# A layered mixture-of-experts and attention kernel: zero fills placed earlier in SP's queue, and the order of scores, value products, maxima and quotient in the attention loop

## The chip, the cores and the metric

The kernel runs on one core of one Trainium2 chip. The metric is the device time of one execution in microseconds (us). A core has five engines with a queue of instructions each: TensorE (PE in the profile, with its weight loads as PEld), VectorE (DVE), ScalarE (ACT), GpSimd (POOL) and SyncE (SP). SP does no arithmetic here; it issues transfers, which 16 DMA engines carry out. Engines wait for each other by semaphores.

## The reference, cut to what matters

There are 32 sequences of 128 tokens with 128 channels, so 4096 tokens, and a condition vector of 64 values for each sequence. Two layers follow each other, each with a residual:

```
x = x + ffn0(cond0(x, cond))     # cond0: channels scaled by the condition, a product, clip
x = x + ffn1(cond1(x, cond))     # cond1: adapter 128 -> 32 -> 128 with conditioned weights
ffn0: router, the best 2 of 8 experts (silu gated, width 176), and a shared expert
ffn1: h = layernorm(x); q, k, v = h @ w_qkv
      scores = q k / sqrt(8), 16 heads of 8 channels;  attn = softmax(scores)
      x = x + (attn v) @ w_o + b_o
      h = layernorm(x); router, the best 2 of 8 experts (relu, width 512)
      x = x + experts
```

## The kernel before, in words

The program has five stages, one after the other: `layer0` (condition, shared expert and router of the first layer, 0 to about 115 us), `experts0` (the first layer's routed experts, to 237), `pre_attention` (adapter, layer norm, q, k, v, to 306), `attention` (with the second router, to about 545), and `experts1` (to the end). All are written engine by engine: each stage has one function for each engine, and the order of its queue is the order of the calls there. Nothing is planned by a scheduler.

**Routing through DRAM.** A router writes each token's row into a DRAM buffer of 8 regions, one for each expert (`dispatch_rows` for the first layer, `late_rows` for the second), by scatters from GpSimd. The experts then read tiles of 256 rows, in 39 tiles. As the last tile of an expert is not full, unused rows must be zero. `fill_region` (L404) writes zeros over one region of `late_rows` with two DMAs of 1040 KB on SP's queue, and `fill_dead` (L415) over what lies past the regions with one. Of the 8 regions, `layer0` fills the first six (`EARLY_FILLS`, L399 to L412, called at L559), and SP fills the last two in `attention`, at pairs 2 and 3 (L1656). The semaphore `m.filled` counts all of them. GpSimd waits for the full count at lap 10 of `attention` (L1706), before its first scatter into `late_rows`.

**The end of `experts0`.** For each tile SP loads the rows and the weights (L1002, L1004). GpSimd scatters the expert's result rows into `expert_rows` (L948, `send_rows`). A tile may take its result buffer only when the scatters of four tiles before have landed (L932). Behind the last tile's loads SP issues two loads of the adapter's gains (`gbu`, L1006; the trace names them `eg`) and then calls `fetch_halves` (L855): it waits for the scatters that concern the first half of `expert_rows`, loads it into V with four DMAs of 512 KB, waits for the rest, and loads the second half into X3 with four more (L865). VectorE waits for all four loads of V, adds V onto X in eight instructions (L956), and adds X3 for the first two groups of four sequences (L964). Then the stage ends for all engines, and the first instruction of TensorE in `pre_attention` (L1339) can start.

**The attention loop.** One lap handles one sequence s; a lap runs over four groups g of four heads. In lap s TensorE does, for each g:

* `score(s + 2, g)` (L1884): masked keys times queries, for the maxima;
* `shift(s, g)` (L1894 and L1896): keys times queries again, minus the maximum, for the exponent;
* at g = 0 `mix(s - 1)` (L1914): the value products, 32 small matmuls into psO; at g = 3 `total(s - 1)` (L1923): the sums of the exponents, 32 more;
* at g = 0 the ranks for the router, once in four laps (`post_rank`, L266); at g = 1 `turn_max(s + 1)` (L1902), a transpose of the maxima, or at g = 2 in the lap with `routing`; at g = 2 or 3 `project(s - 2)` (L1933).

VectorE takes the maxima (`maximum`, L1735, four a lap), spreads them (`spread_max`, L1741), computes the reciprocal of the sums (`invert`, L1747), the quotient (`divide`, L1752) and the residual (`keep`, L1756). The score banks are two, so `score(s, g)` waits for the maximum of g - 2. GpSimd splits the maxima into two parts (`part_max`, L1680 and L1682), masks keys (`mask_k`, L1670), spreads values (`spread_v`, L1690) and scatters rows (L358). ScalarE takes the exponents (L1833) and masks keys (L1826).

**Norm and router** of a group of four sequences run in pieces in later laps, so every fourth lap has the same piece. Six laps behind: VectorE's moments, gather and variance (L1450, L1458, L1466) and GpSimd's root (L1473). Seven: offset, norm and its transpose. Eight: GpSimd's join (L1480), the product for the router (L1522). Nine ("routing"): logits and the choice of experts on VectorE. Ten ("placing"): ranks, slots and the index (L339), then GpSimd's scatters, two a lap for four laps.

SP's queue in `attention` loads queries and keys a pair of sequences at a time (`load_pair`, L1129, three buffers) and the masked queries (`load_masked`, L1594), each behind a wait for `shifted`.

Of the kernel before, what the change touches and what calls it, by code (L numbers as in the profile page):

```python
# [17 lines left out]
SEQS = 32  # L18
# [4 lines left out]
E = 8  # L23
# [377 lines left out]
EARLY_FILLS = 6  # L401


def fill_region(m, sp, e):  # L404


    tiles = TOK // SLOTS // FILLS
    rows = m.tail[:, e].rearrange("p a c -> p (a c)").unsqueeze(1).to_broadcast([P, tiles, 2 * ROW])
    for f in range(FILLS):
        at = e * REGION + f * tiles * SLOTS  # L410
        sp.dma_start(m.xbufs[1][at:at + tiles * SLOTS].rearrange("(i p a) c -> p i (a c)", p=P, a=2), rows
                     ).then_inc(m.filled, 16)  # L412
# [444 lines left out]
def fetch_halves(m, sp, sent, layer):  # L857


    for a, to in enumerate((m.V, m.X3)):  # L860
        sends_done(m, sp, sent, layer, a)
        mine = m.ybuf[a * TOK:(a + 1) * TOK, :].rearrange("(p s) c -> p s c", s=SEQS)
        for h in range(HALVES):
            part = slice(h * HS1, (h + 1) * HS1)
            sp.dma_start(to[:, part, :], mine[:, part, :]).then_inc(m.rows_in[1 + h] if a else m.rows_in[0], 16)  # L865
# [101 lines left out]
def experts0(m, d):  # L967

    nc = m.nc
    with ExitStack() as ctx:  # L970
# [4 lines left out]
        s = [sb(f"es{q}", [HALF, 2, SLOTS]) for q in range(2)]  # L975
# [15 lines left out]
        with nc.Block(no_gpsimd_drain=True) as block:  # L991
            @block.sync
            def _(sp):
                for n, b, i in rounds(sp, ETILES, EB, head=EB, tail=EB - 1):
                    if isinstance(n, int) and n < LEAD:
                        continue
                    e = sp.value_load(m.table[0:1, bass.ds(n, 1)], min_val=0, max_val=E - 1)
                    row = sp.value_load(m.table[0:1, bass.ds(n + ETILES, 1)], min_val=0, max_val=E * REGION + (E - 1) * SLOTS)
                    hold(m, sp, down, n - EB + 1)
                    hold(m, sp, copied, n - EB + 1)  # L1000
                    hold(m, sp, evac, n - EB + 1)
                    sp.dma_start(xs[b][:], m.xbufs[0][bass.ds(row, SLOTS), :].rearrange("(a p) c -> p a c", p=P)  # L1002
                                 ).then_inc(ld[b], 16)
                    sp.dma_start(w[b][:], d["W123"][bass.ds(e, 1)].rearrange("e p h -> (e p) h")  # L1004
                                 ).then_inc(ld[b], 16)
                for b in range(2):  # L1006
                    sp.dma_start(gbu[b][:], m.gb_dram[b * GT:(b + 1) * GT, 2 * DOWN:].unsqueeze(0).to_broadcast(
                        [DOWN, GT, 2 * P])).then_inc(m.gbu_in[b], 16)
                fetch_halves(m, sp, st, 0)

            @block.tensor
# [515 lines left out]
def post_logits(q, dve, n, b, banks):  # L1527

    route_logits(q.router, dve, n, b, banks, q.nat)
# [74 lines left out]
def attention(m, d):  # L1604
# [3 lines left out]
    with ExitStack() as ctx:  # L1608
# [33 lines left out]
        with nc.Block(no_gpsimd_drain=True) as block:  # L1642
            @block.sync
            def _(sp):
                for k in range(PAIRS):
                    ahead = k + 1
                    if 2 <= ahead < PAIRS:
                        if ahead >= PAIR_BUFFERS:
                            sp.wait_ge(shifted, HG * 2 * (ahead - PAIR_BUFFERS + 1))
                        if ahead % 2 == 0:  # L1650
                            sp.wait_ge(m.qk_out[ahead // 2 % 2], 16 * (ahead // 4 + 1))
                        load_pair(m, sp, ahead, ahead % PAIR_BUFFERS)
                    if k >= 2:
                        sp.wait_ge(shifted, HG * 2 * (k - 1))
                        load_masked(m, sp, k)
                    if k in (2, 3):  # L1656
                        fill_region(m, sp, EARLY_FILLS + k - 2)
                sp.wait_ge(mixed, SEQS)
                lead_weights(m, sp, tiles, d["W1b"], m.late_w)
                lead_rows(m, sp, tiles, 16 * (FILLS * E + 1),  # L1660
                          [(sem, post.router.sends * GROUPS // 2) for sem in post.router.scattered], m.xbufs[1], m.late_xs)
# [66 lines left out]
            def _(dve):  # L1728
# [39 lines left out]
                for s in range(LAPS):  # L1768
                    if s == 8:
                        stores_landed(m, dve)  # L1770
                    inner = 2 <= s < SEQS + 2
                    varying, centring, routing, placing = (group(s, k) for k in (6, 7, 9, 10))
                    if s + 2 < SEQS:
                        maximum(s + 2, 0)
                    if varying is not None:
                        post_moments(post, dve, varying, kept)
                    if centring is not None:
                        post_centre(post, dve, centring)
                    if routing is not None:
                        post_logits(post, dve, routing, routing % 2, post.natural_banks)  # L1780
                    if inner:
                        invert(s - 2)
                    if s + 2 < SEQS:
                        maximum(s + 2, 1)
                    if varying is not None:
                        post_gather(post, dve, varying)
                    if placing is not None:
                        index_slot(r, dve, placing, post.rank_out)
                    if inner:
                        divide(s - 2)  # L1790
                    if routing is not None:
                        choose_best(r, dve, routing)
                    if s + 2 < SEQS:
                        maximum(s + 2, 2)
                    if varying is not None:
                        post_variance(post, dve, varying)
                    if routing is not None:
                        choose_expert(r, dve, routing)
                    if placing is not None:
                        index_place(r, dve, placing, post.rank_out)  # L1800
                    if s + 1 < SEQS:
                        spread_max(s + 1)
                    if s + 2 < SEQS:
                        maximum(s + 2, 3)
                    if routing is not None:
                        choose_hot(r, dve, routing)
                    if placing is not None:
                        index_sum(r, dve, placing)
                    if inner:
                        keep(s - 2)  # L1810
                    if routing is not None:
                        choose_mask(r, dve, routing)
# [58 lines left out]
            def _(pe):  # L1871
# [73 lines left out]
                for s in range(LAPS):  # L1945
                    behind, inner = 1 <= s < SEQS + 1, 2 <= s < SEQS + 2
                    turning, scaling, routing, placing = (group(s, k) for k in (7, 8, 9, 10))
                    for g in range(HG):
                        if s + 2 < SEQS:
                            score(s + 2, g)  # L1950
                        if s < SEQS and (s > 0 or g > 1):
                            shift(s, g)
                        if behind and g == 0:
                            mix(s - 1, range(4))
                        if behind and g == 3:
                            total(s - 1, range(4))
# [263 lines left out]
```

## Time and profile before

| | us |
|---|---|
| median of 3 runs | 696.9 (695.83 to 698.49) |
| the profiled execution, whole | 700.72 |
| its span, first to last instruction | 698.9 |
| PE busy | 593.7 (85%) |
| DVE busy | 473.7 (68%) |
| POOL busy | 433.3 (62%) |
| ACT busy | 389.3 (56%) |

The profiled execution lies 3.8 us above the median of the runs; times inside a stage come from it. Busy shares are of the whole span; the stages have different limits. A matmul's end is modelled, so the start of an instruction is the more reliable end of its row. Idle time is written behind a row in brackets, with what ended it. The program's numbered buffers and names that end in a number are shown without it: X3 appears as X.

### The profile page before, as it was taken

To read this page: it belongs to the slowest core of one execution; us is meant where nothing else is said; L and a number is where in the kernel's file an instruction comes from. 1 tells how busy PE (TensorE), PEld (TensorE's weight loads), DVE (VectorE), ACT (ScalarE), POOL (GpSimd) and SP (SyncE) were. 2 spreads that over 40 slices of the span, in tenths; PEclk is the share of its full clock that TensorE was granted. 3 is DMA by queue.
4 is the path that set the end of the run, shared out by engine and by line. 5 is a ranking of instruction groups with operands and counts; after the bars stand their busy time and mean duration, and the time that the engine had idled before them with its cause. 6 is when DMAs were issued, how large, how long until landed. Compare 5 with 4: busy or idle time off the path is not lost.

```text
span 698.9 us, 17755 instructions
## 1 busy us (share of the span) xinstructions
PE 593.7 (85%) x5559; PEld 475.7 (68%) x5559; DVE 473.7 (68%) x1514; ACT 389.3 (56%) x841; POOL 433.3 (62%) x573
## 2 busy tenths in 40 slices
PE   4999953999998378869999999999961699999996
PEld 2566632988998256536766766766741599999993
DVE  3665552766777367756878788879745478888874
ACT  3544401655555068776777777778641355555551
POOL 2677760666677565534454878977777155666663
PEclk9999995999999589967999999999985699999999
DMA  7999996767677518561873443443113798888858
GB/s 224 249 203 297 288 260 145 196 205 198 202 224 226 202 39 247 205 203 55 251 202 87 111 125 105 127 126 85 47 36 98 220 300 269 251 249 252 246 186 267
DMA packets 106298, 131.23 MB, mean 188 GB/s; under 512 B 16272, under 2 KB 83888, under 8 KB 106096
## 3 DMA queue, kind: packets, MB, share of 16 engines
q1 hardware_dynamic: 92864, 109.40, 57.1%
q0 software_dynamic: 9088, 18.76, 8.2%
q10 hardware_dynamic: 4272, 2.14, 1.0%
q8 instruction: 39, 0.64, 0.4%
q14 instruction: 35, 0.29, 0.1%
HBM read 80.75 MB, written 49.50 MB: 186 GB/s over the span
## 4 chain that ended last, share of the span: by engine, by line
PE 29%; POOL 12%; issue 9%; DVE 2%; DMA 2%; ACT 1%; SPq 1%; ACTq 0%; POOLq 0%; DVEq 0%
PE psO L2058 10%; PE psA L939 8%; POOL late_rows L358 7%; PE ps L1884 2%; PE ps L1894 2%; PE ps L1896 2%; POOL vb L1690 2%; PE psAO L1914 2%; PE psAO L1923 1%; PE psT L889 1%; POOL X L1480 1%; POOL rstd L1473 1%; DMA kp<-qk_parts 1%; POOL xmx L1682 1%; SPq L1129 1%
## 5 line engine op out<-in xcount | busy, mean ns | idle before, releaser
L948 POOL DMA_INDIRECT expert_rows<-fo,to x78 | 84.6, 1085 | 62.5 <-DVE fo L2081 49.1
L1735 DVE TENSOR_REDUCE mneg<-ps 128x4 f32<-128x512 f32 x128 | 86.2, 676 | 41.4 <-PE ps L1884 39.9
L948 POOL DMA_INDIRECT expert_rows<-eo,to x78 | 75.1, 962 | 53.9 <-ACT eo L1094 34.2
L1833 ACT ACTIVATE arena<-ps 128x512 f32<-128x512 f32 x128 | 75.5, 590 | 49.8 <-PE ps L1896 48.8
L358 POOL DMA_INDIRECT dispatch_rows<-row,index x64 | 62.4, 976 | 34.4 <-issue 19.2
L921 DVE CAST xh<-psT 128x256 fp32r<-128x256 f32 x78 | 33.1, 424 | 66.6 <-PE psT L889 65.9
L358 POOL DMA_INDIRECT late_rows<-row,index x64 | 63.9, 998 | 20.3 <-issue 15.1
L939 PE MATMUL psA<-xh,wh 128*128 128x256 f32 (+1 forms) x234 | 73.3, 313 | 1.4 <-DVE xl L925 1.4
L1826 ACT ACTIVATE km<-kp,const 96x512 fp32r<-96x512 f32 x96 | 67.7, 712 | 3.4 <-PE ps L1884 1.3
L1884 PE MATMUL ps<-km,qp 96*128 96x512 f32 x128 | 63.4, 502 | 4.8 <-ACT km L1826 3.6
L939 PE MATMUL psA<-xh,wl 128*128 128x256 f32 (+1 forms) x234 | 66.9, 286 | 0.0
L939 PE MATMUL psA<-xl,wh 128*128 128x256 f32 (+1 forms) x234 | 66.7, 285 | 0.0
L1670 POOL TENSOR_SCALAR km<-kp,const 96x512 fp32r<-96x512 f32 x32 | 50.1, 1565 | 15.1 <-POOLq L1180 10.2
L2058 PE MATMUL psO<-wb,fh 128*128 128x128 f32 x464 | 56.4, 275 | 0.3 <-ACT fh L2140 0.3
L2058 PEld LDWEIGHTS psO<-wb,fh 128*128 128x128 f32 x464 | 54.3, 192 | 0.5 <-ACT fh L2140 0.5
L1894 PE MATMUL ps<-qm,kp 96*128 96x512 f32 x128 | 52.6, 411 | 0.9 <-DVE mxT L1741 0.5
L1896 PE MATMUL ps<-mxT,selr 128*128 128x512 f32 x128 | 51.7, 404 | 0.0
L939 PEld LDWEIGHTS psA<-xh,wh 128*128 128x128 f32 (+1 forms) x234 | 42.7, 182 | 2.3 <-DVE xl L925 2.2
L939 PEld LDWEIGHTS psA<-xl,wh 128*128 128x128 f32 (+1 forms) x234 | 42.8, 183 | 0.0
L939 PEld LDWEIGHTS psA<-xh,wl 128*128 128x128 f32 (+1 forms) x234 | 42.6, 182 | 0.0
L1884 PEld LDWEIGHTS ps<-km,qp 96*128 96x128 f32 x128 | 25.6, 201 | 19.4 <-issue 11.5
L2129 ACT ACTIVATE fw<-psO,xt 128x128 f32<-128x128 f32 x58 | 18.2, 365 | 33.7 <-PE psO L2058 27.2
(232 smaller groups left out, 1570.6 us busy)
## 6 DMA issues: line engine op xcount, KB each, us to landing
late_rows<-tail SPq DMA_DIRECT2D x17, 1040.0 KB, 18.4
wb<-in_W1b SPq DMA_DIRECT2D x29, 578.0 KB
w<-in_W SPq DMA_DIRECT2D x29, 304.0 KB
qk_parts<-qk SPq DMA_DIRECT2D x8, 1024.0 KB, 4.7
qp<-qk_parts SPq DMA_DIRECT2D x48, 128.0 KB
kp<-qk_parts SPq DMA_DIRECT2D x48, 128.0 KB
qm<-qk_parts SPq DMA_DIRECT2D x192, 32.0 KB
arena<-in_W1b SPq DMA_DIRECT2D x10, 578.0 KB
```

Of the source, the lines that this page charges most:

```text
L358: pool.indirect_dma_start(out=r.xbuf, out_offset=bass.IndirectOffsetOnAxis(ap=r.index[b][:, c:c + 1], axis=0), in_=r.row[b][:, c // TOPK, ...
L921: v.tensor_copy(z.xh[q][:], z.psT[:, q, 0:SLOTS]).then_inc(z.x_high, 1)
L939: ins = z.m.nc.tensor.matmul(out, w[k][q][:, columns], x[k][q][:], start=(k == 0), stop=(k == 2), skip_group_check=True)
L948: pool.indirect_dma_start(out=m.ybuf, out_offset=bass.IndirectOffsetOnAxis(ap=to[b][:, a:a + 1], axis=0), in_=out[b][:, a, :], in_offset=N ...
L1670: ins = nc.gpsimd.tensor_scalar(km[s % 2][:, :, j, :], kp[side(s)][:, :, tok(s)].bitcast(F32), mask(j), None, ALU.mult)
L1735: nc.vector.tensor_reduce(mneg[s % 2][:, g, :], ps1[:, g % 2, :].rearrange("p (j k) -> p j k", j=4), AX_X, ALU.max, negate=True).then_inc( ...
L1826: nc.scalar.activation(km[s % 2][:, :, j, :], kp[side(s)][:, :, tok(s)].bitcast(F32), ACT.Copy, scale=mask(j)).then_inc(km_act, 1)
L1833: nc.scalar.activation(prob[s % 2][:, g, :], ps2[:, g % 2, :], ACT.Exp, scale=ATT_SCALE).then_inc(exped, 1)
L1884: nc.tensor.matmul(ps1[:, g % 2, :], qp[side(s)][:, g, tok(s)], km[s % 2][:, g].rearrange("p j k -> p (j k)"), start=True, stop=True).then ...
L1894: nc.tensor.matmul(ps2[:, g % 2, :].rearrange("p (j k) -> p j k", j=4), kp[side(s)][:, g, tok(s)], qm[(s // 2) % 2][:, g, :, tok(s)], star ...
L1896: nc.tensor.matmul(ps2[:, g % 2, :], selr[:, g, :], mxT[s % 2][:].rearrange("p j k -> p (j k)"), start=False, stop=True).then_inc(shifted, 1)
L2058: ins = nc.tensor.matmul(psO[:, q, a * P:(a + 1) * P], h[q][:, k, a * P:(a + 1) * P], wb[b][:, WIDE + k * P:WIDE + (k + 1) * P], start=(k ...
```

## The change

It does three things.

* The fills of the last two regions of `late_rows` (four DMAs) leave SP's queue in `attention` and go to SP's queue in `experts0`, behind the two loads of gains and ahead of `fetch_halves`.
* On TensorE the value products of `mix(s - 1)` move from g = 0 to g = 1 of the lap, so `score(s + 2, 1)` and `shift(s, 1)` stand ahead of them. The ranks of the router stay at g = 0.
* On VectorE `maximum(s + 2, 1)` moves ahead of `invert(s - 2)`, and `divide(s - 2)` follows `invert` at once, ahead of the gather of the moments and of the slot of the index; before, they and the maximum stood between.

```diff
--- before.py
+++ after.py
@@ -1006,6 +1006,8 @@
                 for b in range(2):
                     sp.dma_start(gbu[b][:], m.gb_dram[b * GT:(b + 1) * GT, 2 * DOWN:].unsqueeze(0).to_broadcast(
                         [DOWN, GT, 2 * P])).then_inc(m.gbu_in[b], 16)
+                for e in range(EARLY_FILLS, E):
+                    fill_region(m, sp, e)
                 fetch_halves(m, sp, st, 0)
 
             @block.tensor
@@ -1653,8 +1655,6 @@
                     if k >= 2:
                         sp.wait_ge(shifted, HG * 2 * (k - 1))
                         load_masked(m, sp, k)
-                    if k in (2, 3):
-                        fill_region(m, sp, EARLY_FILLS + k - 2)
                 sp.wait_ge(mixed, SEQS)
                 lead_weights(m, sp, tiles, d["W1b"], m.late_w)
                 lead_rows(m, sp, tiles, 16 * (FILLS * E + 1),
@@ -1778,16 +1778,15 @@
                         post_centre(post, dve, centring)
                     if routing is not None:
                         post_logits(post, dve, routing, routing % 2, post.natural_banks)
+                    if s + 2 < SEQS:
+                        maximum(s + 2, 1)
                     if inner:
                         invert(s - 2)
-                    if s + 2 < SEQS:
-                        maximum(s + 2, 1)
+                        divide(s - 2)
                     if varying is not None:
                         post_gather(post, dve, varying)
                     if placing is not None:
                         index_slot(r, dve, placing, post.rank_out)
-                    if inner:
-                        divide(s - 2)
                     if routing is not None:
                         choose_best(r, dve, routing)
                     if s + 2 < SEQS:
@@ -1950,7 +1949,7 @@
                             score(s + 2, g)
                         if s < SEQS and (s > 0 or g > 1):
                             shift(s, g)
-                        if behind and g == 0:
+                        if behind and g == 1:
                             mix(s - 1, range(4))
                         if behind and g == 3:
                             total(s - 1, range(4))
```

## Rows read from the trace of the kernel before

**Rows 1.** Busy time by stretch: PE, PEld, DVE, ACT, POOL; clock, DMA share, GB/s.

```profile
370.00:510.00 140.00, 133.66 (x1918) 96.26 (x1916) 113.84 (x390) 105.01 (x202) 108.90 (x208) 1.00 0.37 101
```

**Rows 2.** Timeline of SP, end of the first expert stage: start, duration, instruction, count.

```profile
215.12 0.92 SPq L1007 DMA_DIRECT2D eg<-cond_rows  x2
221.37 1.77 SPq L865 DMA_DIRECT2D V<-expert_rows  x4
229.05 1.79 SPq L865 DMA_DIRECT2D X<-expert_rows  x4
```

**Rows 3.** Timeline of DVE, POOL and PE around that end; in brackets idle before.

```profile
219.41 0.17 DVE L932 COPY to<-xs 128x2 uint32<-128x2 uint32 x1 [0.88 <-DMA expert_rows<-eo,to]
...
230.45 4.91 DVE L956 TENSOR_TENSOR X<-V,X 128x512 f32<-128x512 f32 x8 [2.93 <-DMA V<-expert_rows]
...
230.18 0.95 POOL L948 DMA_INDIRECT expert_rows<-eo,to  x1 [0.31 <-issue]
...
237.68 1.08 PE L1339 MATMUL psX<-const,X 128*128 128x128 f32 x4 [9.62 <-PEq L991]
```

**Rows 4.** Busy time in the hole of the DMA engines, as rows 1.

```profile
218.00:222.00 4.00, 4.00 (x38) 4.00 (x37) 3.10 (x10) 2.19 (x6) 3.05 (x4) 1.00 0.24 86
```

**Rows 5.** Fills at the front: SP's timeline, landing times, DMA queues of 59:92.

```profile
59.05 31.71 SPq L411 DMA_DIRECT2D late_rows<-tail  x7
...
DMA to landing us min/median/max: 17.7/18.7/21.9
...
q1 hardware_dynamic: 7644, 7.82, 90.4%
q0 software_dynamic: 834, 1.74, 18.2%
```

**Rows 6.** Fills in attention: SP, DMA rates in 40 slices of 345:362, chain, waits.

```profile
345.82 1.03 SPq L411 DMA_DIRECT2D late_rows<-tail  x2
...
GB/s 80 164 104 137 238 322 350 340 321 330 335 333 343 338 352 338 321 259 259 242 313 360 258 294 287 203 222 145 210 101 92 104 94 96 109 106 68 2 0 0
...
353.41 5.84 DMA kp<-qk_parts
...
359.28 0.72 ACT L1826 ACTIVATE km<-kp,const 96x512 fp32r<-96x512 f32 x1 [0.77 <-DMA kp<-qk_parts]
...
359.34 1.57 POOL L1670 TENSOR_SCALAR km<-kp,const 96x512 fp32r<-96x512 f32 x1 [3.01 <-DMA kp<-qk_parts]
```

**Rows 7.** Timeline of PE, early laps of attention.

```profile
339.74 1.08 PE L1914 MATMUL psAO<-arena,vb 128*32 128x128 f32 x32
340.75 0.50 PE L1884 MATMUL ps<-km,qp 96*128 96x512 f32 x1
341.08 0.40 PE L1894 MATMUL ps<-qm,kp 96*128 96x512 f32 x1
341.32 0.40 PE L1896 MATMUL ps<-mxT,selr 128*128 128x512 f32 x1
...
346.31 0.50 PE L1884 MATMUL ps<-km,qp 96*128 96x512 f32 x1
```

**Rows 8.** Timelines of POOL, PE and DVE in one period; last the chain.

```profile
405.55 1.06 POOL L1473 TENSOR_TENSOR rstd<-var,minus_half 128x4 f32<-128x4 f32 x1 [1.38 <-DVE var L1466]
...
410.54 0.28 PE L1902 MATMUL psM<-const,xmx 128*32 128x128 f32 x1 [1.25 <-POOL xmx L1682]
...
421.60 0.95 DVE L1747 RECIPROCAL rec<-psAO 128x128 f32<-128x128 f32 x1
422.67 0.69 DVE L1735 TENSOR_REDUCE mneg<-ps 128x4 f32<-128x512 f32 x1
...
430.83 1.13 POOL rstd L1473
```

**Rows 9.** Scatters into DRAM, with and without fills beside them: us to landing.

```profile
dispatch_rows<-row,index POOLq DMA_INDIRECT x64, 7.7
...
late_rows<-row,index POOLq DMA_INDIRECT x64, 2.7
```

## The prediction

> **What bounds the kernel now.** I read the stages first, then the two places that the change touches. The attention stage, from 306 to about 510 us, is bounded by a ring of three engines and not by one. In its early laps (a lap is one sequence) TensorE is never idle: the second score of one lap starts at 340.75 and that of the next at 346.31, so 5.56 us each [rows 7]. Later, in every fourth lap, GpSimd waits 1.38 us for VectorE's variance, and TensorE waits 1.25 us for GpSimd's split maxima [rows 8]; GpSimd's root starts at 405.55 and again at 430.83, a period of 25.28 us for four laps [rows 8]. TensorE is busy for 133.7 of 140 us there, at a granted clock of 1.00, so 2.4 GHz [rows 1]. So little can be won: the ring gives way only where one of its engines is late.
>
> The place to look at is the end of the first expert stage. VectorE has finished its small work by 227.5 (230.45 less its wait) and then waits 2.93 us for the loads of V; the eight additions on V start at 230.45 and take 4.91 us, two on X follow, and TensorE, idle for 9.62 us, starts the next stage at 237.68 [rows 3]. V's four loads are issued at 221.37, X's four at 229.05, both by SP [rows 2]. Whatever delays V delays everything after it, one for one; nothing else in the kernel covers it.
>
> **The change, part by part.**
>
> **The fills.** Four zero fills of 1040 KB (1.065 MB) leave SP's queue between the attention loads and enter it at 216.0, behind the two loads of the adapter's gains and ahead of V's [rows 2]. As instructions they cost little: four issues of about 0.5 us (two take 1.03 in the attention stage [rows 6]), done by 218.1, over 3 us before V's issue at 221.37. Their bytes are another matter. The DMA engines are used only 0.24 between 218 and 222, at 86 GB/s [rows 4]. A hole of 4 us takes at most 1.4 MB at the 340 GB/s or so that the later fills reach [rows 6]; 4.26 MB don't fit. Then the question is whether V's reads pass them. The traces say no. At the front, seven fills issued back to back took 31.71 us of SP's time, 4.53 us each, and the fills landed a median 18.7 us after their issue, so four of them stand in line, and SP is held for the time of one [rows 5]. In the attention stage kp's loads, issued behind two fills, landed 5.84 us after their last issue, though they are 128 KB each [rows 6]. So V goes behind the fills.
>
> The Trainium skill ("DMA: Bandwidth & Descriptors", Queues, rings and completion order) has each engine consume one queue's descriptors in ring order, SP's being one queue; the rows agree, and the rule speaks against putting anything large ahead of V.
>
> How long they take: the nearest row is the front's, as there too GpSimd scatters rows all the while: SP's queue moved 7.82 MB in 33 us (59 to 92) beside 1.74 MB of scatters [rows 5], 237 GB/s or 4.5 us a fill. Here the scatters end at 231.1 [rows 3]. From 218.0, three fills at 4.53 end at 231.6, the fourth at 340 GB/s at 234.7. V's four loads of 512 KB, 2.1 MB, take 9.0 us now from issue to landing [rows 2, 3], of which 6.2 are moving at 340 GB/s; in a line the start is covered, and I keep 0.5 for the landing. So V is there at 241.4 in place of 230.4: **+11.0 us**. The fast end has all four fills at 340 GB/s (12.5 us): V at 237.2, +6.8. The slow end has all four at 4.53 and V at its whole 9.0: 245.1, +14.7. X's loads come behind V's, the first of them 2 us after; VectorE needs it only 4.9 us after V [rows 3], so X adds nothing.
>
> The Trainium skill (the same page, Bandwidth) gives 341 GB/s for 1 MB transfers into SBUF. By that figure, as an estimate, the fills cost the fast end, +6.8; the front's row, with scatters beside the fills, says 4.53 us each, and I go by the row.
>
> What the removal gives back: ScalarE waited 0.77 us and GpSimd 3 us for kp, until 359.3 [rows 6]. The chain of waits runs from kp through ScalarE's masks and normalised rows to TensorE, so ScalarE's wait is what counts: **-0.8 us**, between 0 (something else is late) and -3.0 (all of GpSimd's). GpSimd's wait for the fills at lap 10 costs nothing on either side; they have landed long before.
>
> **TensorE's order.** The value products, 32 matmuls in 1.01 us (339.74 to 340.75 [rows 7]), now stand behind the second score and its shifted score. All work before the turn of the maxima is still before it. What is saved is a bubble: a score behind the value products starts its shift 0.33 us later, against 0.24 from shift to shift [rows 7]. In laps where the turn follows the products, that is 0.09 us saved, and in the routing lap of four nothing. Eight laps bound by TensorE give 0.7. In the ring, TensorE's stretch between the turn at 410.54 and the first score of the routing lap holds one such lap: 0.09 a period. The rank products now come about 1 us sooner, and may wait some 0.1 us for VectorE's mask; TensorE has 1.25 us of slack in the next lap for that.
>
> **VectorE's order.** The second maximum goes ahead of the reciprocal and the quotient. The same instructions stand before the variance, so its time moves only by idle time: after the reciprocal at 421.60, which ends at 422.55, the second maximum starts at 422.67, 0.12 us of waiting that goes away, as its score comes 1 us sooner [rows 8]. The quotient ends at about the same time, since it no longer has the second maximum between it and the reciprocal. 0.12 + 0.09 over five periods is 1.05, with the 0.7 above **-1.8 us**. Bounds: +1.0, if the new rank wait and a later quotient each cost 0.1 in the periods, and -7.4, if GpSimd's 1.38 us wait went wholly in five periods and the 0.7 stayed at 0.5 or so.
>
> **Sum.** 11.0 - 0.8 - 1.8 = +8.4 us. The profiled execution took 700.72 (span 698.9), so 709.1 on its own terms. It lies 3.8 above the median of the runs, 696.9; so I predict 705.3.
>
> **Rivals.**
> **A, the expert stage ends late as well.** Scatters beside fills landed in 7.7 us, without them in 2.7 [rows 9]. VectorE already waits 0.88 us for one at 219.41 [rows 3]. If the last three tiles each wait 5 us more, the stage ends up to 15 us late, 4 beyond V: +12.4, 709.3. For it: that wait is there now. Against: each tile waits for a send four tiles back, which GpSimd's backlog has mostly issued before 218. The Trainium skill (same page, Queues, rings and completion order) says that the engines take turns between queues by packets, which is why sends would be slowed and not stopped.
> **B, a fast drain.** 340 GB/s in spite of the scatters: +6.8 - 0.8 - 1.8 = +4.2, 701.1. For it: the attention stage's fills. Against: the front's row.
> **C, not slower.** V's reads are not held by the fills, at the one place 221.4 to 230.4: 0 - 0.8 - 1.8 gives 694.3. It decides if 4.26 MB are out of V's way when its reads begin, about 223, which is 850 GB/s from 218.0, or if reads pass writes in the same queue. The chain through kp speaks against both.
> **D, the new order frees the ring.** GpSimd's 1.38 us wait goes in each of five periods: +11.0 - 0.8 - 7.4 = +2.8, 699.7. Against: VectorE has the same work ahead of the variance in either order.
>
> **How the numbers follow.** Forecast 0.60 (own range 702.5 to 708), A 0.14, B 0.12, C 0.09, D 0.05. A measurement of this kernel can tell about 0.5%, 3.5 us, from no change: slower is above 700.4. Slower is the forecast, A and three quarters of B, 0.83; within 0.5% the rest of B, D and half of C, 0.13; faster 0.04. The range from 699 to 710.5 leaves out C and the far tails.
>
> **What would show it.** V's additions start at about 241 and the adapter's first product at about 248.5, where they were 230.45 and 237.68; the DMA rate is near 300 GB/s from 218 to 241; at 216 stand four issues of late_rows. In the attention stage, kp no longer stands in the chain, the early lap is 5.47 us, and the period 25.07. Wrong would be: V's additions before 236 (then B or C), a period under 24.5 (D), the last expert product after 235 (A).

## The result, and the profile after

The changed kernel took 705.2 us (median of 16 executions, 701.39 to 707.49), the kernel before 696.7 us in the same series (16 executions, 694.27 to 702.83). The ratio is 1.0117, with a 95% interval of 1.0097 to 1.0136, so the change costs 8.2 us (6.8 to 9.5). The profiled execution of the changed kernel took 707.49 us, its span is 705.7. The forecast was 705.3. The total came out right with two terms wrong that stand against each other, so its closeness is partly luck: less was lost at the expert stage than I said, and almost nothing was won in the attention stage.

From the page of the changed kernel; line numbers differ from before by up to 3.

```profile
## 1 busy us (share of the span) xinstructions
PE 599.3 (85%) x5559; PEld 483.3 (68%) x5559; DVE 476.3 (67%) x1514; ACT 389.0 (55%) x841; POOL 433.8 (61%) x573
```

**The end of the first expert stage.** These answer to [rows 2, 3]. First SP's timeline in the changed kernel:

```profile
210.07 0.93 SPq L1007 DMA_DIRECT2D eg<-cond_rows  x2
211.04 7.50 SPq L411 DMA_DIRECT2D late_rows<-tail  x4
223.55 3.79 SPq L865 DMA_DIRECT2D V<-expert_rows  x4
230.27 1.75 SPq L865 DMA_DIRECT2D X<-expert_rows  x4
```

Then VectorE's and TensorE's timelines there:

```profile
214.36 0.17 DVE L932 COPY to<-xs 128x2 uint32<-128x2 uint32 x1 [1.11 <-DMA expert_rows<-eo,to]
...
219.18 0.17 DVE L932 COPY to<-xs 128x2 uint32<-128x2 uint32 x1 [2.93 <-DMA expert_rows<-eo,to]
...
222.25 0.17 DVE L932 COPY to<-xs 128x2 uint32<-128x2 uint32 x1 [2.27 <-DMA expert_rows<-eo,to]
...
235.44 4.91 DVE L956 TENSOR_TENSOR X<-V,X 128x512 f32<-128x512 f32 x8 [8.96 <-DMA V<-expert_rows]
...
242.29 1.09 PE L1341 MATMUL psX<-const,X 128*128 128x128 f32 x4 [14.96 <-PEq L991]
```

Times of day can't be compared, as the stages ahead of this one took 5 us less in this execution; the last load ahead of the change, that of the gains, is the common mark. From there to the additions on V it is 230.45 - 215.12 = 15.3 us before [rows 2, 3] and 235.44 - 210.07 = 25.4 after: **10.0 us more**. To the adapter's first product it is 22.6 before and 32.2 after, 9.7 more. The wait for V is 8.96 us long in place of 2.93.

V's first load is issued 13.5 us behind the gains in place of 6.3, and from there to the additions it takes 11.9 us in place of 9.1.

Busy time by stretch in the changed kernel, the stretches being the fills and the loads behind them (columns as in rows 1):

```profile
211.00:228.30 17.30, 11.86 (x83) 10.63 (x81) 8.74 (x23) 5.90 (x15) 11.28 (x12) 0.78 1.07 324
228.30:235.40 7.10, 0.00 (x0) 0.00 (x0) 0.00 (x0) 0.00 (x0) 0.08 (x1) 0.50 1.02 404
```

The bytes of SP's queue (q1) alone, from 213.3 to 228.3:

```profile
q1 hardware_dynamic: 4178, 4.36, 95.1%
```

The DMA engines are full all the way. The boundary at 228.3 is read from the packets of SP's queue: those of the fills have 1040 bytes, those of V and X 4096, and nearly all of the fills' move between 213.3 and 228.3. Ahead of them the queue still moves the loads issued before. So the four fills were out 17.3 us after their first issue, 15.0 us of it for their own bytes, and V took 7.1 us more. They landed at 218.2, 222.5, 226.5 and 230.2, some 4.0 us apart. The granted clock is 0.50 (1.2 GHz) while TensorE is idle, as it was in the kernel before (0.51 from 228.1 to 237.6), and the next stage isn't longer: from its first product to the first score 70.5 us before, 69.8 after.

**The attention stage.** TensorE's early lap, GpSimd's root, VectorE's maximum, reciprocal, quotient and variance, and TensorE's rank product in the changed kernel, for [rows 7, 8]:

```profile
345.79 0.49 PE L1883 MATMUL ps<-km,qp 96*128 96x512 f32 x1
346.11 0.40 PE L1893 MATMUL ps<-qm,kp 96*128 96x512 f32 x1
...
351.26 0.48 PE L1883 MATMUL ps<-km,qp 96*128 96x512 f32 x1
...
408.79 1.06 POOL L1475 TENSOR_TENSOR rstd<-var,minus_half 128x4 f32<-128x4 f32 x1 [1.43 <-DVE var L1468]
...
434.11 1.06 POOL L1475 TENSOR_TENSOR rstd<-var,minus_half 128x4 f32<-128x4 f32 x1 [1.46 <-DVE var L1468]
...
424.01 0.69 DVE L1735 TENSOR_REDUCE mneg<-ps 128x4 f32<-128x512 f32 x1 [1.75 <-PE ps L1883]
...
425.38 0.95 DVE L1747 RECIPROCAL rec<-psAO 128x128 f32<-128x128 f32 x1
426.36 0.29 DVE L1752 TENSOR_TENSOR oT<-psAO,rec 128x128 f32<-128x128 f32 x1
...
431.73 0.94 DVE L1747 RECIPROCAL rec<-psAO 128x128 f32<-128x128 f32 x1
432.69 0.29 DVE L1752 TENSOR_TENSOR oT<-psAO,rec 128x128 f32<-128x128 f32 x1
...
433.86 0.16 DVE L1468 TENSOR_SCALAR var<-mv 128x4 f32<-128x4 f32 x1
...
430.08 0.17 PE L266 MATMUL psW<-mask,tri 128*128 128x8 bf16 x1 [0.15 <-issue]
```

In the kernel before, the same waiting maximum and the variance that ends the stretch:

```profile
420.83 0.69 DVE L1735 TENSOR_REDUCE mneg<-ps 128x4 f32<-128x512 f32 x1 [1.75 <-PE ps L1884]
430.60 0.15 DVE L1466 TENSOR_SCALAR var<-mv 128x4 f32<-128x4 f32 x1
```

The early lap is 351.26 - 345.79 = 5.47 us, as forecast. The period of four laps, from one root to the next, is 434.11 - 408.79 = 25.32 us against 25.28 before [rows 8]; I had forecast 25.07. ScalarE's wait for kp is gone, and of GpSimd's 0.2 us are left. From the first score of the stage to the last scatter it is 234.0 us before and 233.3 after, 0.7 less, where 2.6 less was forecast. The rest of the difference of the two spans lies in stages that the change doesn't touch: those ahead took 5.0 us less, the last one 3.7 more (151.7 us before, 155.4 after). In the kernels of series 2 and 3 below, none of which changes it, the last stage took 151.5 to 153.9 us.

### The profile page after: what moved, and what is told of

It is laid out like the page before. It is cut to its first block and busy times, and to the rows that moved or that the text cites. A ratio compares the mean times of both kernels' runs of the same rounds, so it can differ in the third digit from the quotient of the medians.

```text
span 705.7 us, 17755 instructions
## 1 busy us (share of the span) xinstructions
PE 599.3 (85%) x5559; PEld 483.3 (68%) x5559; DVE 476.3 (67%) x1514; ACT 389.0 (55%) x841; POOL 433.8 (61%) x573
## 5 line engine op out<-in xcount | busy, mean ns | idle before, releaser
L358 POOL DMA_INDIRECT dispatch_rows<-row,index x64 | 62.4, 976 | 35.5 <-issue 19.2
L358 POOL DMA_INDIRECT late_rows<-row,index x64 | 63.9, 998 | 20.4 <-issue 15.1
L1883 PE MATMUL ps<-km,qp 96*128 96x512 f32 x128 | 61.7, 488 | 4.9 <-ACT km L1825 3.6
L2128 ACT ACTIVATE fw<-psO,xt 128x128 f32<-128x128 f32 x58 | 18.1, 364 | 34.0 <-PE psO L2057 26.3
L1913 PE MATMUL psAO<-arena,vb 128*32 128x128 f32 x1024 | 35.4, 280 | 0.0
```

The costliest lines, as they stand in the source:

```text
L358: pool.indirect_dma_start(out=r.xbuf, out_offset=bass.IndirectOffsetOnAxis(ap=r.index[b][:, c:c + 1], axis=0), in_=r.row[b][:, c // TOPK, ...
L1883: nc.tensor.matmul(ps1[:, g % 2, :], qp[side(s)][:, g, tok(s)], km[s % 2][:, g].rearrange("p j k -> p (j k)"), start=True, stop=True).then ...
L1913: nc.tensor.matmul(psO[32 * g:32 * g + 32, p, 0:P], vb[p][:, 4 * g + j, :], prob[p][:, g, j * P:(j + 1) * P], start=(j == 0), stop=(j == 3 ...
```

## Experiments

Two theories had to be told apart for each place. **F**: the loss is the fills' place in SP's queue ahead of V's loads; with the fills elsewhere it is gone. Against it, that the new order costs, or that the 4.26 MB cost the same wherever they are written. **D**: in the attention stage TensorE's new order gives what it should and VectorE's takes it back, through the quotient right behind its reciprocal. Against it, that neither order does anything, or that both are needed together.

### Series 1: each part alone

This series ran where the kernel before itself took 771.4 us; the first expert stage alone took some 25 us longer in its profiles. Only differences inside the series are used. The fills alone, with the order as before:

```diff
@@ experts0, SP
+                for e in range(EARLY_FILLS, E):
+                    fill_region(m, sp, e)
                 fetch_halves(m, sp, st, 0)
@@ attention, SP
-                    if k in (2, 3):
-                        fill_region(m, sp, EARLY_FILLS + k - 2)
```

> Only the fills move; TensorE's and VectorE's order is that of before. Theory F (the fills' bytes and SP's time in issuing them hold V up, all of the loss is theirs): slower than before by 9 us, from 8 to 10: V's additions start about 25 us after the load of the adapter's gains (15.3 before), and the first part of attention gains 0.8 us from kp's earlier loads. Rival O (a good part of the loss is the new order in attention): slower by 5 us or less.

Measured: ratio 1.0052 (1.0018 to 1.0086), 4.0 us. By this number F's 8 to 10 us missed, and it lies in O's range. The new orders alone, with the fills as before:

> Only the order on TensorE and VectorE changes; the fills stay in attention. Theory F: within 1 us of before, as the period of four laps is 25.31 us against 25.28 and the early lap 5.47 against 5.56. My forecast's step said -1.8 us. Rival O: slower by 3 us or more.

Measured: 1.0007 (0.9973 to 1.0041), so the order doesn't cost what O needs, 3 us or more, though 3 us is just inside the interval. There the gains' load to the adapter's first product took 26.5 us with the fills in the attention stage and 32.0 with the fills ahead of V: 5.5 more, about half of what the main comparison shows; V's loads were issued 10.2 us behind the gains there even without the fills, against 6.3.

The fills in `pre_attention`, order as before:

```diff
@@ pre_attention, SP
                 for n, b, i in unrolled(GROUPS, 2):
+                    if n == 1:
+                        for e in range(EARLY_FILLS, E):
+                            fill_region(m, sp, e)
                     if not first(n):
                         store(n - 1, 1 - b)
```

> The four fills go into the stage behind, pre_attention, ahead of the first store of q and k, where the DMA engines moved 26 GB/s from 236 to 260 us; order as before. If the fills cost only where other loads are in line behind them, this keeps the 0.8 us of attention and loses nothing: faster than before by 0.5 to 1.5 us. If four fills cost something wherever they are (SP held for 7.5 us, ahead of the store at 259.5), equal or slower by 1 to 3 us.

Measured: 0.9974 (0.9942 to 1.0006), with a period of 26.5 us. And the same with TensorE's new order alone:

> As the run before, with TensorE's new order and VectorE's old one. Theory D (in the changed kernel the quotient stands directly behind the reciprocal and waits 0.12 us for its result, twice a period; that ate the gain): without it the period is 25.07 us, and the early lap 5.47; about 2 us faster than before in all. Rival: the period stays at 25.28 or above, since VectorE's second maximum behind the reciprocal is what matters: then within 1 us of the run before.

Measured: 0.9981 (0.9949 to 1.0012), with a period of 26.9, so longer, not shorter. With an interval of 0.3% on each, and all periods 1.1 us or more longer than in the main comparison, this pair decides nothing about the order; it was tried again in series 3.

### Series 2: the same parts where the kernel before took 701.5 us

> The kernel of e1_fills_only once more, as the first series ran on a chip where before itself took 771 us, not 697. If before takes about 697 here: theory F says slower by 8 to 10 us (ratio 1.012 to 1.014), with V's additions about 25 us after the load of the adapter's gains against 15.3. If the loss were shared with the new order, it would be 5 us or less.

Measured: **1.0120 (1.0094 to 1.0147)**, the whole loss, as F expected. SP's timeline with the fills alone:

```profile
215.40 0.90 SPq L1007 DMA_DIRECT2D eg<-cond_rows  x2
216.35 8.23 SPq L411 DMA_DIRECT2D late_rows<-tail  x4
229.62 2.99 SPq L865 DMA_DIRECT2D V<-expert_rows  x4
```

Gains to additions 25.4 us, to the adapter's first product 32.2, both as in the changed kernel.

> The kernel of e2_order_only once more, for the same reason. Theory F: within 1.5 us of before, period 25.31 us. Rival O (the order costs): slower by 3 us or more. My forecast's step: faster by 1.8 us.

Measured: 1.0006 (0.9987 to 1.0026), period 25.32. The forecast of the two orders together, -1.8 us or 0.9974, is outside the interval. The product of both parts, 1.0126, is inside the interval of the whole change.

Half of the fills at the new place, the other half in the attention stage:

```diff
@@ experts0, SP
+                fill_region(m, sp, EARLY_FILLS)
                 fetch_halves(m, sp, st, 0)
@@ attention, SP
-                    if k in (2, 3):
+                    if k == 3:
```

> Only region 6 is filled at the end of the first expert stage (two DMAs, 2.1 MB), region 7 stays in attention; order as before. Theory F (the cost goes with the bytes that stand ahead of V, less what the hole of the DMA engines takes): V's additions 3 to 5 us later than before, counted from the load of the gains, and slower by 2.5 to 4.5 us in all. Rival P (what costs is the place: anything issued there costs the same): nearly the whole 9 us. If the hole of 4 us took 1.4 MB and SP was not held: about 2 us.

Measured: 1.0040 (1.0015 to 1.0065). SP's timeline with half of the fills:

```profile
214.05 0.90 SPq L1007 DMA_DIRECT2D eg<-cond_rows  x2
214.99 1.12 SPq L411 DMA_DIRECT2D late_rows<-tail  x2
224.59 1.79 SPq L865 DMA_DIRECT2D V<-expert_rows  x4
```

Two fills hold SP for 1.12 us only, four for 7.50 or 8.23. V's additions come 19.2 us after the gains, 3.9 more than before, for 2.1 MB. But V's loads are still issued 4.2 us later than before (10.5 us behind the gains against 6.3), though SP's issues are short: SP waits here for the scatters into `expert_rows`, which land late beside the fills. SP's waits ahead of V's loads, first with half of the fills, then in the kernel before (us in total, times, longest us):

```profile
SPq L875 <- DMA expert_rows<-eo,to: 4.9, 2, 3.1
SPq L875 <- DMA expert_rows<-eo,to: 2.6, 1, 2.6
```

From their first issue V's loads then take 8.7 us to the additions, as before (9.1). So in this kernel the 3.9 us come through the late issue: the fills' last packets move at about 225, just as V's first load is issued (224.59), and little of V stands behind them.

The repair that I took for best: the fills in `pre_attention` as in series 1, TensorE's new order, and on VectorE the quotient moved back behind other work.

```diff
                     if s + 2 < SEQS:
                         maximum(s + 2, 1)
                     if inner:
                         invert(s - 2)
-                        divide(s - 2)
                     if varying is not None:
                         post_gather(post, dve, varying)
                     if placing is not None:
                         index_slot(r, dve, placing, post.rank_out)
                     if routing is not None:
                         choose_best(r, dve, routing)
+                    if inner:
+                        divide(s - 2)
```

> The fills in pre_attention, TensorE's new order, and VectorE's new order with one difference: the quotient stands behind the gather, the slot and the choice of the best, so that something lies between it and the reciprocal. Theory D (the 0.12 us gap between reciprocal and quotient ate the gain): period 25.07 us, early lap 5.47; in all 2 us faster than before or a little more. Rival: period 25.28 or above; then 1 us or less.

Measured: **0.9954 (0.9936 to 0.9973)**, faster than both kernels; periods 25.07, 25.03, 24.98 and 24.97. The quotient has other work ahead of it in two laps of four; in the others it still stands directly behind its reciprocal (0.97 us), and the period doesn't show that. The two faster kernels, this one and the one with TensorE's order alone in series 3, can't be told apart.

### Series 3: where the fills can stand, and which order does it

The kernel before took 697.1 us here. First the fills in `pre_attention`, order as before:

> The four fills issued in pre_attention (SP's second iteration there) and every order as before. Theory F (what the change cost is the fills' place ahead of V's loads and SP's hold on them) expects the load of the gains to V's loads at 6.3 to 6.9 us and V's loads to the additions at 8.6 to 9.0, as before, the attention stage without the wait for kp, so the first root to the second about 24.7, its period unchanged at 25.3, and the ratio 0.998 to 1.000. Rival: moving the fills costs the same wherever they stand, since their 4.26 MB delay some load; it expects pre_attention 3 us or more longer and 1.004 or more.

Measured: **0.9972 (0.9955 to 0.9989)**, a little better than F's 0.998 to 1.000. SP's timeline with the fills in `pre_attention`:

```profile
210.08 0.92 SPq L1007 DMA_DIRECT2D eg<-cond_rows  x2
216.47 1.77 SPq L865 DMA_DIRECT2D V<-expert_rows  x4
224.05 1.76 SPq L865 DMA_DIRECT2D X<-expert_rows  x4
232.21 0.80 SPq L1185 DMA_DIRECT2D gbu<-cond_rows  x2
233.05 6.26 SPq L411 DMA_DIRECT2D late_rows<-tail  x4
254.00 0.37 SPq L1191 DMA_DIRECT2D qk_parts<-qk  x1
```

The same bytes and a hold of 6.26 us, and nothing waits for it: SP's next issue is 15 us later. Gains to additions 15.2 us, as before. The rival, that the bytes cost the same anywhere, falls.

The same with TensorE's new order, VectorE's as before:

```diff
-                        if behind and g == 0:
+                        if behind and g == 1:
                             mix(s - 1, range(4))
```

> As the kernel above, and on TensorE the value products behind the second score and shift; VectorE's order is as before. Theory D (the shorter path through TensorE is worth 0.1 to 0.2 us a period, and VectorE's new order gave it back by a quotient standing right behind its reciprocal) expects a period of 25.1 to 25.2 and a ratio 0.001 under the kernel above. Rival P (TensorE's new order gives nothing alone, since the second maximum, behind reciprocal and its 0.12 us, is still what sets the ring; both orders are needed together) expects 25.3 or more and no difference to the kernel above. If P holds, all of the gain of 0.3 us a period of the spread order is VectorE's or the pair's.

Measured: **0.9945 (0.9924 to 0.9967)**, 3.8 us faster than before, periods 24.98 to 25.02 where the kernel above has 25.27 to 25.29. Rival P, that TensorE's order gives nothing alone, falls by these periods; the times, 695.3 and 693.9 us, have intervals that overlap. The gain a period is larger than D said (25.1 to 25.2). VectorE's and GpSimd's timelines with TensorE's new order alone:

```profile
415.04 0.69 DVE L1736 TENSOR_REDUCE mneg<-ps 128x4 f32<-128x512 f32 x1 [1.75 <-PE ps L1885]
...
415.81 0.94 DVE L1748 RECIPROCAL rec<-psAO 128x128 f32<-128x128 f32 x1
416.67 0.63 DVE L1736 TENSOR_REDUCE mneg<-ps 128x4 f32<-128x512 f32 x1
...
422.06 0.93 DVE L1748 RECIPROCAL rec<-psAO 128x128 f32<-128x128 f32 x1
422.92 0.62 DVE L1736 TENSOR_REDUCE mneg<-ps 128x4 f32<-128x512 f32 x1
...
424.61 0.15 DVE L1469 TENSOR_SCALAR var<-mv 128x4 f32<-128x4 f32 x1
...
399.82 1.06 POOL L1476 TENSOR_TENSOR rstd<-var,minus_half 128x4 f32<-128x4 f32 x1 [1.08 <-DVE var L1469]
...
424.84 1.07 POOL L1476 TENSOR_TENSOR rstd<-var,minus_half 128x4 f32<-128x4 f32 x1 [1.14 <-DVE var L1469]
```

From the reciprocal to the next start it is 0.86 us here both times; in the changed kernel, where the quotient is next, 0.98 and 0.96.

The fills behind all loads of V and X (`fetch_halves` first, then the loop over `fill_region`):

> The four fills at the same end of the first expert stage, but behind all loads of V and X; every order as before. Theory F expects V's additions 15 to 16 us behind the load of the gains, as before. What stands behind the fills in SP's queue is the start of pre_attention: if TensorE's first product there doesn't wait for SP, the ratio is 0.998 to 1.001; SP issues its first loads of that stage some 7 us later than before, and if one of them is late, that much of it shows, at most 5 us or 1.007. Rival (the fills' bytes slow whatever reads are under way, as the DMA engines share between all outstanding transfers) expects V's additions 3 us or more later and 1.005 or more.

Measured: 1.0053 (1.0033 to 1.0072). SP's and TensorE's timelines:

```profile
218.35 1.77 SPq L865 DMA_DIRECT2D V<-expert_rows  x4
225.81 1.77 SPq L865 DMA_DIRECT2D X<-expert_rows  x4
227.63 11.49 SPq L411 DMA_DIRECT2D late_rows<-tail  x4
...
239.79 1.08 PE L1341 MATMUL psX<-const,X 128*128 128x128 f32 x4 [14.74 <-PEq L991]
```

V's additions start 15.1 us behind the gains and those on X 20.1 us (20.4 before), so V and X are not slowed: the rival in which the fills slow whatever loads are under way falls for loads issued ahead of them. But SP is held for 11.49 us, to 239.12, and only then does the stage end for all engines: TensorE starts at 239.79, 27.7 us behind the gains against 22.6. The loss is SP's hold, through the end of the stage, and not the bytes; I had named it as possible, at up to 5 us.

The fills between the two halves (the same loop inside `fetch_halves`, behind V's loads):

> The four fills between V's four loads and X's four; every order as before. Theory F expects V's additions 15 to 16 us behind the load of the gains, as before, and then VectorE waits for X's first loads: they are issued 5 to 7 us later than before and stand behind 4.26 MB, so they land 10 to 13 us later than before, of which VectorE's additions on V cover about 2 to 3: the stage ends 8 to 10 us later, less than with the fills ahead of V, ratio 1.007 to 1.013. Rival (only a small part of X is needed at once, and V is what the stage waits for) expects under 1.003.

Measured: 1.0155 (1.0129 to 1.0181), the largest loss measured; its interval just reaches the upper end of what F expected, 1.013, and overlaps with that of the fills ahead of V in series 2. In the traces the adapter's first product comes 34.1 us behind the gains here and 32.2 with the fills ahead of V. SP's and VectorE's timelines:

```profile
216.25 1.80 SPq L865 DMA_DIRECT2D V<-expert_rows  x4
218.09 11.37 SPq L411 DMA_DIRECT2D late_rows<-tail  x4
234.42 1.93 SPq L865 DMA_DIRECT2D X<-expert_rows  x4
...
225.40 4.90 DVE L959 TENSOR_TENSOR X<-V,X 128x512 f32<-128x512 f32 x8 [3.59 <-DMA V<-expert_rows]
241.26 1.29 DVE L967 TENSOR_TENSOR X<-X 128x512 f32<-128x512 f32 x2 [10.76 <-DMA X<-expert_rows]
```

I had put SP's hold at 5 to 7 us; it is 11.37, since V's 2.1 MB stand in the queue too. To it come 5.0 us for the four counts that SP reads ahead of the next half. So X's loads are issued 16.4 us behind V's last, against 5.9 before [rows 2], and VectorE waits 10.76 us. The 5.9 were not SP's own time: 2.9 were, and 3.0 a wait for a scatter. Without fills in the queue a read of a count takes SP 0.27 us; here the four take 0.67 to 0.95 us.

## Why the prediction was right or wrong

**The fills' issues (wrong, and it didn't matter).** I said four issues of 0.5 us, done 3 us before V's issue, from the pair in the attention stage [rows 6]. Two fills behave so (1.12 us); four held SP for 7.5. V's issue came 13.5 us behind the gains, not 6.3. The step that failed is the reading of a price of two as a price of four: the front's row [rows 5], which I used for the drain, already showed that SP is held once enough is in line. It cost nothing here as far as the rates tell: the DMA engines were full throughout, and the fills' bytes were out only at 228.3, 4.7 us after V's first issue, so an earlier issue would have put V behind the same bytes. No run separates the two. The scatters would have kept V's issue late as well: the one that SP waits for in the half change landed 9.2 us behind the gains there, and 9.1 behind them in the changed kernel (VectorE's wait that ends at 219.18), after which SP has two more counts to read, 1.3 to 2.5 us by these kernels' reads.

**The fills' bytes (right in mechanism, 1.0 too large at V).** I said that V goes behind the fills, that three of these take 4.53 us each beside scatters and the fourth 3.1. The forecast has 2.0 us from the first issue to the drain, 16.7 for the fills and 6.7 for V, 25.4 in all; measured are 2.3, 15.0 and 7.1, 24.4 in all. So +10.0 in place of +11.0, and the term that was too large is the 4.53 us, which measured 3.75 by the packets. The half change gives +3.9, but by SP's wait for scatters rather than by V in line behind bytes, so it doesn't confirm a price by the byte. The Trainium skill ("DMA: Bandwidth & Descriptors", Queues, rings and completion order) says that each DMA engine consumes descriptors of one queue in ring order; the runs agree with that: V is late when the fills are ahead and on time when they are behind. By its figure of 341 GB/s for 1 MB (an estimate) the fills would have cost +6.8. From 213.3 to 228.3 all queues together moved 331 GB/s, near it, but SP's queue alone 4.36 MB, 291 GB/s (the fills' 4.26 MB make 284), between that figure and the front's 237 [rows 5].

**Rival A (half right).** The sends were slowed: VectorE's waits for them are 1.11, 2.93 and 2.27 us, in place of a longest one of 0.88 [rows 3], and TensorE's last expert product ends 17.3 us behind the gains (242.29 - 14.96 - 210.07) in place of 12.9 [rows 2, 3]. But V came later still, and VectorE's wait for V covered it. It was a mechanism, without a price of its own in the changed kernel. In the half change, where V's bytes were sooner out, it does show, as SP's wait.

**The fills gone from the attention stage (right, within what can be told).** Forecast -0.8. From the first to the second root it was 25.6 before and 24.5 after; with the order of before and all fills away it is 24.7 to 24.8 in all four kernels of series 2 and 3 that have it so: -0.9. With the new order and the fills still there it is 26.0, so there the fills cost 1.5. ScalarE's wait for kp goes with it: 0.77 us before [rows 6], 1.48 with the new order and the fills there. In the half change, where the two fills of pair 3 stay, ScalarE doesn't wait, GpSimd waits 1.7 us, and the stretch is 24.7: GpSimd's wait alone costs nothing, as I had said. Over the whole stage the four kernels with the old order and no fills in it took 233.0, 233.7, 234.0 and 233.0 us against 234.0, so 0 to 1.0 less.

**TensorE's order (the right sign, too small).** I had 0.09 us a period for the bubble, and 0.12 for VectorE's wait behind the reciprocal, which I put down to VectorE's order. Both come from TensorE's order alone: period 25.28 to 25.00. The steps, taken between the maximum that waits for its score and the variance: 9.77 us before (420.83 to 430.60), 9.57 with TensorE's order alone (415.04 to 424.61). The wait was not 0.12 but 1.07 - 0.86 = 0.21: I measured from the end of the reciprocal's record (0.95 us long), though the next instruction can start 0.86 us after it [rows 8]. In the rest of the period, from the variance to the waiting maximum, 15.51 us became 15.47: the bubble, 0.04 where I had 0.09.

**VectorE's order (wrong, the step that failed).** I said that the same instructions stand ahead of the variance, so that nothing but idle time changes, and that the quotient ends at the same time. The instructions are the same, but the quotient now needs the result of the instruction right ahead of it, and starts 0.96 to 0.98 us after it in place of 0.86. It happens twice between the waiting maximum and the variance (425.38 and 431.73), +0.22 in the changed kernel, where the stretch is 424.01 to 433.86 = 9.85 us: 0.28 more than with TensorE's order alone. 0.22 of the 0.28 is this gap; the rest, 0.06, is spread in steps of 0.01 and 0.02 that I can't name. My bound of +0.1 for a later quotient was too small, and the 0.28 takes back all that TensorE's order gave. That the gap is the cause is borne out by the spread order: with other work between the two at both places its stretch is 9.5 to 9.6 us, as with TensorE's order alone. The rank product waited 0.15 us, where 0.1 was forecast; it stands in the same place in the kernels with a period of 25.00, so it isn't what took the gain. With TensorE's order and VectorE's old one the period is 25.00 and with the spread order 25.01, so the second maximum ahead of the reciprocal does nothing that these periods show.

The sum: the stage of the experts +9.7 (forecast +11.0), the attention stage -0.7 (forecast -2.6), together +9.0, against +8.4 forecast and +8.2 measured. The two errors, 1.3 and 1.9, stand against each other and left 0.6. What stays open: the early laps' 0.7 us can't be seen, since the stretch from the first score to the first root varies from 46.2 to 47.3 us in kernels of one order, though the early lap read above is 5.47 us, as forecast; and where the rest comes from of the 2.0 us (0.8 to 3.1) that the fills in `pre_attention` save, when the attention stage shows only 0.4 of it.

**Rivals B, C and D.** B's rate (340 GB/s in spite of the scatters) was nearly reached for all queues together, but not for the fills alone; its additions would have come 237.2 - 215.1 = 22.1 us behind the gains and the forecast's 241.4 - 215.1 = 26.3; they came at 25.4. C fell with V's issue at 223.55 and its landing behind the fills. D fell: GpSimd's wait for the variance is 1.43 us, not zero.

## What to carry to other kernels

Ask of a large transfer that nobody waits for not only whether it is needed soon, but what its queue carries next and what the issuing engine must do next: here the same four fills cost 8.4 us ahead of V, 10.8 between V and X, 3.7 behind both and nothing (2.0 gained) in the second turn of the next stage's loop. The first two intervals overlap. A price per issue read from two transfers isn't the price of four: add up what will stand in the queue, and place the long hold where the engine has nothing to do. And do not put an instruction right behind the one whose result it reads if something independent can stand between; in this ring two such places took back all that the other half of the edit had won.

## What the runs showed of the hardware that I had not expected

* SP's hold depends on what stands in the queue. Four fills of 1.065 MB, issued into a queue with little in it, took 6.26, 7.50 and 8.23 us, two took 1.12, and four behind 2.1 MB of V or X took 11.37 and 11.49. In the first of these the rate of all queues was 315 GB/s over the hold, so at most 2.0 of the 4.26 MB had moved when SP came free and at least 2.3 MB stood in line (an estimate from these rows). What is counted, bytes or packets, no run tells.
* With the loads of V and X (packets of 4096 bytes) in SP's queue all queues together moved 404 GB/s (228.3 to 235.4, the last scatters among them), with the fills and scatters 331 (213.3 to 228.3). The Trainium skill gives 341 GB/s for 1 MB and 425 for 16 MB in "DMA: Bandwidth & Descriptors", Bandwidth; these eight loads of 512 KB back to back, 4.2 MB, lie between.
* A read of a count from SBUF took SP 0.27 us in the kernel before, and 0.87 to 0.89 us in the changed one right behind the four fills. Four such reads stand ahead of V's loads, so SP needed 5.0 us there, where it needed 2.7 before beside a wait of 2.6 for a scatter.
* On VectorE an instruction behind a reciprocal of 128x128 starts 0.86 us after it if it doesn't read its result, and 0.96 to 0.98 if it does. The Trainium skill ("VectorE: DVE Perf Modes", The DRAIN you can't avoid) reports of eight copies in a row that a semaphore behind each costs nothing extra; here the instruction that waits on the reciprocal's semaphore and reads its result starts about 0.11 us later. Whether it is the semaphore or the result, no run tells.
